# Two narrow steps in front, the top network in chunks, and another order of GpSimd's products and gathers

## The reference

```python
e = stack([tbl_f[ids[:, f]] for f in range(32)], axis=1)      # (1024, 32, 16)
x0 = xk = e
for W in (W0, W1, W2):                                        # (32, 32 or 64, 64)
    xk = relu(einsum('bmd,bhd,mhk->bkd', x0, xk, W))          # (1024, 64, 16)
    outs.append(sum(xk, axis=2))                              # (1024, 64)
h = concatenate(outs + [dense_ctx], axis=1)                   # (1024, 208)
h = maximum(h @ W_top1 + b_top1, 0)                           # 512
h = maximum(h @ W_top2 + b_top2, 0)                           # 256
y = h @ W_top3                                                # (1024, 1)
```

## Time and profile before

| | us |
|---|---|
| median of 3 runs (637.17 to 637.77) | 637.69 |
| the profiled execution | 638.89 |
| its span in the trace | 637.1 |
| DVE busy | 548.7 |
| PE busy | 563.1 |
| GpSimd busy | 488.3 |
| ACT busy | 302.5 |

### The profile page before, as it was taken

The page is one execution under the profiler, slowest core; times in us unless marked ns, Lnnn a source line. Parts: engine busy times, 40 slices in busy tenths (PEclk is TensorE's granted clock), DMA queues, the critical chain, the costliest instruction groups (busy, mean ns, idle before and its releaser), DMA issues.

```text
span 637.1 us, 7625 instructions
## 1 busy us (share of the span) xinstructions
PE 563.1 (88%) x2440; PEld 178.9 (28%) x2440; DVE 548.7 (86%) x330; ACT 302.5 (47%) x1359; POOL 488.3 (77%) x364
## 2 busy tenths in 40 slices
PE   0058998999999998999899999999999989999998
PEld 0012232332323232332223232323232322333332
DVE  0038998999999999999999999999999999897810
ACT  0023637354545646364535456464736454544352
POOL 6756898869888888979898788888897989584500
PEclk9997999999999999999999999999999999999999
DMA  3298857677876867686778768686868587871000
GB/s 105 39 391 312 307 200 284 240 298 263 306 274 227 295 217 270 244 299 214 297 274 306 268 238 315 211 298 215 307 213 319 225 302 266 307 284 49 1 1 0
DMA packets 52843, 151.01 MB, mean 237 GB/s; under 512 B 9697, under 2 KB 17377, under 8 KB 52802
## 3 DMA queue, kind: packets, MB, share of 16 engines
q1 hardware_dynamic: 44610, 148.40, 63.6%
q0 software_dynamic: 8192, 2.11, 2.5%
HBM read 147.33 MB, written 3.15 MB: 236 GB/s over the span
## 4 chain that ended last, share of the span: by engine, by line
DVE 36%; PE 24%; DMA 19%; issue 10%; POOL 8%; SPq 2%; ACT 1%; DVEq 0%; POOLq 0%
DVE prod L286 34%; PE y_ps L417 20%; DMA x0bc<-x_rows 15%; POOL emb L247 6%; DVE z L314 2%; DMA emb<-table,row_sb 2%; DMA x_rows<-emb 2%; POOL pool_prod L260 1%; SPq L214 1%; PE x_ps L477 1%; ACT relu L373 1%; PE x0g_ps L477 1%; PE x_ps L470 1%; PE x0g_ps L470 1%; PE x0g_ps L471 1%
## 5 line engine op out<-in xcount | busy, mean ns | idle before, releaser
L286 DVE TENSOR_TENSOR prod<-x0bc,x_ps 128x2048 f32<-128x2048 f32 (+1 forms) x252 | 456.0, 1878 | 8.6 <-ACT x_ps L368 8.6
L417 PE MATMUL y_ps<-prod,w_sb 128*64 128x512 f32 x1640 | 384.9, 599 | 27.8 <-DVE prod L286 27.8
L247 POOL DMA_INDIRECT emb<-table,row_sb x256 | 244.9, 957 | 65.5 <-issue 63.7
L260 POOL TENSOR_TENSOR pool_prod<-x0bc,x_sb 128x1024 f32<-128x1024 f32 x102 | 242.3, 2382 | 45.7 <-ACT x_sb L383 36.3
L417 PEld LDWEIGHTS y_ps<-prod,w_sb 128*64 128x64 f32 x1640 | 115.5, 137 | 280.1 <-issue 219.7
L373 ACT ACTIVATE relu<-y_ps 128x16 f32<-128x16 f32 x512 | 84.5, 287 | 144.3 <-PE y_ps L417 144.3
L368 ACT ACTIVATE x_ps<-y_ps 64x512 f32<-64x512 f32 x128 | 73.0, 570 | 78.5 <-PE y_ps L417 75.8
L417 PE MATMUL y_ps<-pool_prod,w_sb 128*64 128x512 f32 x408 | 105.0, 595 | 1.5 <-POOL pool_prod L260 1.3
L286 DVE TENSOR_TENSOR prod<-x0bc,x0g_ps 128x2048 f32<-128x2048 f32 x32 | 72.6, 2282 | 38.5 <-DMA x0bc<-x_rows 35.3
L373 ACT ACTIVATION_READ_ACCUMULATOR relu<-y_ps 128x1 f32 x512 | 84.7, 315 | 0.2
L383 ACT ACTIVATE x_sb<-relu 64x512 f32<-64x512 f32 x128 | 80.4, 628 | 3.4
(11 more groups left out here) (29 smaller groups left out, 49.2 us busy)
## 6 DMA issues: line engine op xcount, KB each, us to landing
x0bc<-x_rows SPq DMA_DIRECT2D x256, 512.0 KB, 6.8
x0g<-x_rows SPq DMA_DIRECT2D x16, 512.0 KB, 4.7
emb<-table,row_sb POOLq DMA_INDIRECT x256
x_rows<-emb SPq DMA_DIRECT2D x16, 128.0 KB, 2.1
w_sb<-w SPq DMA_DIRECT2D x2, 512.0 KB, 4.6
x_rows<-emb SPq DMA_DIRECT2D x16, 64.0 KB, 2.0
x0bc<-wt SPq DMA_DIRECT2D x1, 512.0 KB, 5.4
x0bc<-wt_a SPq DMA_DIRECT2D x1, 256.0 KB, 4.1
```

Of the source, the lines that this page charges most:

```text
L247: pool.indirect_dma_start(emb[:, turn, DIM * n:DIM * (n + 1)], None, table, bass.IndirectOffsetOnAxis(row_sb[:, at:at + 1], 0)).then_inc(g ...
L260: pool.tensor_tensor(pool_prod[:, n % POOL_RING, :], x0bc[:, slot(s, j), :], x[:], ALU.mult).then_inc(pool_products, 1)
L286: made = dve.tensor_tensor(prod[:, n % RING, 0:count, cols], tiles[:, :, cols], right.unsqueeze(1).to_broadcast([P, count, right.shape[1]] ...
L417: made = pe.matmul(ps[MAPS * h:MAPS * (h + 1), :], w, moving[:, HALF * h:HALF * (h + 1)], start=first, stop=final)
```

## The change

**Steps.** Seventeen steps instead of sixteen: two of 32 rows, then fifteen of 64 (`ROWS_OF`). Every tile, product and matmul of a step takes the step's width. The product's operands get a dimension for the half.

**GpSimd.** Step 0 has no GpSimd products (DVE takes all 16 tiles). Gathers of steps 0, 1 and 2 come first (8, 8, 16). Then each round runs layer 2 of step s and layer 1 of step s+1, with one gather of step s+3 behind each product, and the other gathers of s+3 at the end. PE's positions for these products change with it (`POOL_BEFORE`).

**Top network.** Five chunks: steps 0 to 4, 5 to 8, 9 to 12 (256 rows each), 13 to 15 (192) and 16 (64). Its weights and buffers have room of their own, and the weights are loaded behind step 1's tiles. A chunk's turn is the step behind its last (5, 9, 13, 16): ACT rearranges the sums; PE runs hidden layer 1 before layer 2 of that step, into the x0g banks, hidden layer 2 behind it, and the output behind the first group of the next step's layer 1 (in step 16 between the groups of layer 2); ACT issues the output's DMA. For the last chunk PE contracts the part of layers 0 and 1 first. Layer 2 of the last step is one activation and one DVE sum instead of 32 accumulating activations.

```diff
-STEPS = COLS // PAIR
+ROWS_OF = [32, 32] + [64] * 15
+STEPS = len(ROWS_OF)
-POOL_LAST = {STEPS - 2: (5, 4), STEPS - 1: (5, 4)}
-POOL_COUNT = [POOL_LAST.get(s, (3, 3)) for s in range(STEPS)]
-POOL_BEFORE = {3: [2, 3, 5], 4: [2, 3, 4, 5], 5: [2, 3, 4, 5, 5]}
-GATHERS_AFTER = {1: [1, 1, 8], 2: [1, 1, 4]}
+POOL_OF = {0: (0, 0), STEPS - 2: (5, 4), STEPS - 1: (5, 4)}
+POOL_COUNT = [POOL_OF.get(s, (3, 3)) for s in range(STEPS)]
+POOL_BEFORE = {(1, 0): [], (1, 3): [1, 3, 4], (1, 5): [1, 1, 3, 4, 5],
+               (2, 0): [], (2, 3): [2, 4, 6], (2, 4): [2, 3, 4, 5]}
+AHEAD = 3
...
+CHUNKS = [(0, 5), (5, 9), (9, 13), (13, 16), (16, 17)]
+FINAL = len(CHUNKS) - 1
+TURN = {end: c for c, (_, end) in enumerate(CHUNKS[:FINAL])}
...
@@ SP @@
                 load_x0g(s)
                 load_tiles(s)
+                if s == 1:
+                    for dst, src in ((wt1a_sb[:], wt1_a), (wt1b_sb[:], wt1_b), (wt2_sb[:], wt2), (wt3_sb[:], wt3),
+                                     (bt1_sb[:], bt1), (bt2_sb[:], bt2), (zt_b[MAPS:, :], dense_t)):
+                        sp.dma_start(dst, src).then_inc(mlp_in, 16)
...
@@ GpSimd @@
-            gather(0, 0, GATHERS)
+            gather(0, 0, GATHERS_OF[0])
             pool.wait_ge(rows_done, 2)
-            gather(1, 0, GATHERS)
+            gather(1, 0, GATHERS_OF[1])
+            gather(2, 0, GATHERS_OF[2])
             pool.wait_ge(w0_ready, 2)
             for s in range(STEPS):
-                layer(s, 1, x1_sb)
-                layer(s, 2, x2_sb)
+                done = layer(s, 2, x2_sb, s + AHEAD, 0)
+                if s < LAST:
+                    done = layer(s + 1, 1, x1_sb, s + AHEAD, done)
+                if s + AHEAD < STEPS:
+                    gather(s + AHEAD, done, GATHERS_OF[s + AHEAD])
...
@@ DVE @@
-                made = dve.tensor_tensor(prod[:, n % RING, 0:count, cols], tiles[:, :, cols],
-                                         right.unsqueeze(1).to_broadcast([P, count, right.shape[1]]), ALU.mult)
+                out, left = (t.rearrange("p t (h c) -> p t h c", h=2)[:, :, halves, :]
+                             for t in (prod[:, n % RING, 0:count, 0:width(s)], x0bc[:, at:at + count, 0:width(s)]))
+                right = x[:, halves, 0:half(s)].unsqueeze(1).to_broadcast(list(left.shape))
+                made = dve.tensor_tensor(out, left, right, ALU.mult)
...
@@ ACT @@
             for s in range(STEPS):
+                if s - 1 in TURN:
+                    hidden2(TURN[s - 1])
+                    output(TURN[s - 1])
+                if s in TURN:
+                    mlp_input(TURN[s], range(3))
                 if s < LAST:
                     place_x0g(s + 1)
                     square(s + 1)
                 finish(s, 1, x2_ps, x2_sb)
                 if s < LAST:
                     finish(s + 1, 0, x1_ps, x1_sb)
-                else:
-                    mlp(range(MLP_EARLY))
+                if s in TURN:
+                    hidden1(TURN[s])
+                if s == LAST:
+                    hidden2(TURN[s])
+                    output(TURN[s])
+                    mlp_input(FINAL, range(2))
                 finish(s, 2)
...
@@ PE @@
+            def hidden1(c):
+                n, first = CHUNK_ROWS[c], FIRST_ROW[CHUNKS[c][0]]
+                b = slice(first, first + n)
+                pe.wait_ge(zt_ready, inputs_after(c))
+                for j in range(H1_TILES):
+                    ps, out_f = x0g_ps[:, j // 2, CHUNK_B * (j % 2):][:, 0:n], slice(P * j, P * (j + 1))
+                    pe.matmul(ps, wt1a_sb[:, out_f], zt_a[:, 0:n], start=True, stop=False)
+                    made = pe.matmul(ps, wt1b_sb[:, out_f], zt_b[:, b], start=False, stop=True)
...
+            def output(c):
+                n = CHUNK_ROWS[c]
+                pe.wait_ge(mlp_act, PIECES_OF_CHUNK * c + H1_TILES + H2_TILES)
...
             for s in range(STEPS):
-                layer(s, 1, w1_sb)
+                layer(s, 1, w1_sb, {1: lambda: output(TURN[s - 1])} if s - 1 in TURN else {})
                 if s < LAST:
                     layer0(s + 1)
+                if s in TURN:
+                    pe.wait_ge(mlp_in, 16 * 7)
+                    hidden1(TURN[s])
+                if s == LAST:
+                    layer(s, 2, w2_sb, {2: lambda: hidden2(TURN[s]), 4: lambda: output(TURN[s])})
                 else:
-                    pe.wait_ge(mlp_in, 16 * 7)
-                    mlp(range(MLP_EARLY))
-                layer(s, 2, w2_sb)
-            mlp(range(MLP_EARLY, len(MLP)))
+                    layer(s, 2, w2_sb)
+                    if s in TURN:
+                        hidden2(TURN[s])
+            last_chunk()
```

More of the change, by code:

```diff
@@ L259, in layer @@
                         pool.wait_ge(pool_products_used, n - POOL_RING + 1)
[L260 to L264 removed]
+                    pool.tensor_tensor(pool_prod[:, n % POOL_RING, 0:width(s)], x0bc[:, slot(s, j), 0:width(s)],
+                                       x[:, 0:width(s)], ALU.mult).then_inc(pool_products, 1)
@@ L294, in layer0 @@
                     dve.wait_ge(bc_in[g], 32 * (s + 1))
-                    at = slot(s, group[0])
-                    product(before((s, 0)) + g, GROUP, x0bc[:, at:at + GROUP, :], x0g_ps)
+                    product(s, before((s, 0)) + g, group, x0g_ps)
             def layer(s, l, x):
@@ L301, in layer @@
                         dve.wait_ge(bc_in[g], 32 * (s + 1))
-                    n, at, count = before((s, l)) + g, slot(s, group[0]), len(group)
-                    tiles = x0bc[:, at:at + count, :]
+                    n = before((s, l)) + g
                     if g == 0:
@@ L352, in place_x0g @@
                     act.wait_ge(products, after((s - 1, 0)))
-                act.activation(x0g_ps[:].rearrange("p h c -> p (h c)"), x0g[:], ACT.Copy).then_inc(x0g_placed, 1)
+                act.activation(x0g_ps[:, :, 0:half(s)], x0g[:, 0:width(s)].rearrange("p (h c) -> p h c", h=2),
+                               ACT.Copy).then_inc(x0g_placed, 1)
             def square(s):
@@ L357, in square @@
                     act.wait_ge(squares_used, s)
-                act.activation(squares[:], x0g[:], ACT.Square).then_inc(squared, 1)
+                act.activation(squares[:, 0:width(s)], x0g[:, 0:width(s)], ACT.Square).then_inc(squared, 1)
             def finish(s, l, x=None, x_sb=None):
```

303 lines of the change are left out of this document (179 added, 124 removed).

## The result

The changed kernel takes 670.68 us, median of four runs (668.9 to 680.1), against 637.73 for the kernel before: 1.052 times as long, 95% interval 1.0475 to 1.056. The forecast was 620.2 in a range of 608 to 631. The profiled execution of the changed kernel is its slowest and a disturbed one (680.1 us, span 678.3, where the other three spans are 667.1 to 670.1), so losses read from its trace are too large by 8 to 11 us in all. Beside it I read the trace of e1 (664.75 us, span 663.0), the same program but for 60 bytes of padding.

The account below looks back on a forecast made before the run. DVE was taken as the bound, 34.35 us a step of 64 rows wherever nothing interrupts it. Span 637.1 - 7.3 - 6.7 + 15.0 - 18.5 = 619.6, plus 0.6 gives a median of 620.2 us, range 608 to 631.

Parts of the forecast that it names:

- Part 1, the front: Start of the span: narrow first steps bring layer 2 of step 2 to 97.5 us from 104.79, -7.3 us.
- ACT's spread follows: Step 0, after PE's layer 0 tiles end at 28.6: ACT spreads promptly, so DVE's layer 1 starts at 29.5.
- Part 2, the middle: Steady steps: gathering step s+3 in the round of s removes waits for rows before layer 0, -6.7 us.
- Part 3, the turns: Steps 5, 9 and 13: the top network's PE work delays DVE's layer 2 by 5.0 us each, +15.0 in all.
- Part 4, the end: Behind PE's last layer: 10.0 us remain instead of 28.5, -18.5; the 51.6 us of PE chain before it stay.
- 8 records at the 0.19 of their weight loads 1.5: End, behind the last layer of 64 rows: eight PE records priced at 0.19 us each, 1.5 us.
- 16 records 3.0: End, behind the last layer of 64 rows: sixteen further PE records, 3.0 us.
- the last sentence of that part: End: by the skill's 107 ns a load instead of 190, 24 loads are 2.0 us shorter and the end 8.0.
- B: Rival: PE absorbs the top network in its idle time, each turn costing 1.5 us or less; 609.7 us, chance 0.2.
- C: Rival: GpSimd sets the period, its wait of 1.5 us a step making 34.35 into 35.3; 631.6 us, chance 0.13.
- D: Rival: PE's clock stays slow in front, rising only behind step 0, +7 us; 627 us, chance 0.08.
- E: Rival: slower than before, the product's extra operand dimension costing DVE per instruction; 650.6 us at 100 ns, chance 0.06.

Follow-up runs that it names:

- e5: Changed kernel with GpSimd starting the 16 gathers of step 2 only when x1 of step 0 has been copied; 674.43 us.
- e11: Changed kernel with GpSimd's indirect gathers of all steps but the first replaced by plain DMAs of the same shape from rows in order; 634.21 us.
- e7: Changed kernel with the gathers of steps 5 to 16 left out, reusing rows already in the buffer; 648.99 us.
- e10: Changed kernel with GpSimd's indirect gathers of steps 5 to 16 replaced by plain DMAs of the same shape from rows in order; 650.89 us.
- e14: e11 with the seven loads of the top network's weights behind the tiles of step 3 instead of step 1; 630.70 us.
- e6: Changed kernel with the top network left out for the rows of steps 0 to 12, so without the three middle turns; 655.37 us.
- e3: Changed kernel with GpSimd's gathers placed as in the kernel before; 660.60 us, ratio 1.030 to the kernel before.
- e4: e3 with the offset column given 64 bytes a partition instead of 4; 662.22 us, ratio 1.034 to the kernel before.
- e8: Changed kernel with 16 steps of 64 rows and gathers placed as before, keeping only the chunked top network; 648.77 us, ratio 1.012 to the kernel before.
- e9: e8 with the first three chunks' hidden products cut into four pieces behind layer 0 of four steps; 633.58 us, ratio 0.988 to the kernel before.
- e12: Changed kernel with each step's 16 gathers spread over six GpSimd products as 3, 3, 2, 3, 3, 2; 747.25 us, ratio 1.166 to the kernel before.
- e13: e9 with each step's gathers spread over six GpSimd products as 3, 3, 3, 3, 2, 2; 737.65 us, ratio 1.152 to the kernel before.

## Why the prediction was wrong, point by point

**Part 1, the front: -7.3 forecast, +14.5 found.** DVE's first product was forecast at 24.0 and came at 24.73; the half-width pair at 1.13 us start to start held as well. Layer 1 was forecast at 29.5 and came at 43.91. The failed step is the sentence "ACT's spread follows": it took the 0.2 us of rows 11 and 12 for a place where GpSimd was in a row of 24 indirect gathers. e5 and e11 start layer 1 at 31.2 and 31.3 when that row is gone. The second failure is a size: I let rows be read back 3 to 4 us behind their store, as in the idle queue of rows 8, and they took 4.9 to 6.5. Of the 21.8 us between 97.5 and 119.3, what goes with the indirect DMAs is 8.4 (e11; the same front took 125 in e7 and e10, so up to 14), the weight loads are up to 4.8 (3.3 were in the forecast) and the rest, 8.6, is the narrow steps' own loads and scatter. Narrow steps gain 0.9 us over the kernel before even in e14 (103.9 for 104.8), and nothing in any version with real gathers.

**Part 2, the middle: -6.7 forecast.** What it said of the waits for rows is right: with e7, e10 and e11 there is no wait left in front of layer 0, and 34.35 us stand in row. The step that failed is that it took GpSimd's gathers as something that only occupies GpSimd. Between e11 and the changed kernel, whose only difference is the indirect instruction and its addresses, the middle differs by 36.8 us in the one trace and by 17.6 in e1's (511.0 and 493.4). In the kernel before, the runs are of 8 and 4 and behind a product of each layer; the run of eleven lies across both moments, x2 and x1, at which DVE needs PE's result with 1.3 us to spare. The new order did some harm by itself: with it x2 came up to 7.7 us late (e6 too), with the old places 0.8 at most (e3, e4). In time the old places give only 4 to 10 us back. The new order takes away the wait in front of layer 0 and puts late releases in its place, and the gain of 6.7 us is lost in the exchange.

**Part 3, the turns: 5.0 us each forecast.** Right without gathers: 39.65 - 34.35 = 5.3. Beside real gathers 6.2 to 7.7 (e3, e8) and up to 9.4 (e1), 5.1 to 5.8 each by e6's time.

**Part 4, the end: -18.5 forecast.** Right, in part by luck: 8.0 us behind PE's last layer for 10.0 forecast, and from layer 2 of the last but one step (617.14) to PE's end (670.3) 53.2 for the 51.6 that were to stay. The 2.0 are mostly the terms "8 records at the 0.19 of their weight loads 1.5" and "16 records 3.0": a load of 128 columns still takes 0.19 us, but they start 0.11 us apart, and the records took 1.1 and 2.0. (That is why the 8.0 of the last sentence of that part comes out.) The two misses nearly cancel: 61.2 us in all for 61.7.

**The sum.** Taken without indirect DMAs and with the weights later, the kernel has a span of 627.6 (e14); the forecast was 619.6, and of the 8.0 us between them 6.4 are the front. What GpSimd's indirect DMAs cost is best read from medians: e11 and the changed kernel are 36.5 us apart (634.21 and 670.68; the kernel before took 638.57 and 637.73 beside them). The traces give 29.9 between e11 and e1, namely 10.9 in front, 17.6 in the middle and 1.4 in the rest. The weights' place is worth 3.5 us in medians (e14 against e11). So of the 50.5 us between 620.2 and 670.7 the indirect DMAs are 36.5, the weights 3.5 and what e14 still lacks 10.5, most of it in front.

**The rivals.** B (PE absorbs the network) is wrong for turns of 7.7 us and nearly right for pieces of 1.7 (e9). C looked at GpSimd, the right engine, but for its products' times; e12 and e13 show that this limit is real and close, though not what happened. D did not happen: the clock granted to PE was 1.00 from 43.9 to 65.4, while DVE multiplied layers 1 and 2 of step 0, and where it was lower there (0.86 and then 0.71 in e11) DVE still did both layers without a wait inside. In the middle it doesn't go with the waits stretch by stretch (0.96 in the one above of 34.41 us, 1.00 in that of 41.87); the 0.89 is 10 us at the lower level, from 348.4 on, behind a pause of PE that began at 346.15, so a late release can bring a slower PE with it. E is refuted: eight products of layer 1 with the new operand form take 14.46 us, as in rows 3:

```profile
325.31 14.46 DVE L334 TENSOR_TENSOR prod<-x0bc,x_ps 128x1024 f32<-128x1024 f32 x8
```

The one rival for the slower side was thus a cost per instruction. None looked at what a moved run of gathers does to others, and no row of before could price it: its steady stretches have runs of eight and four and take 34.35 us all the same.

## What to carry to other kernels

A wait that takes 0.2 us in one place of a trace isn't worth 0.2 us everywhere: look at what the other engines issue at that moment, and take a second trace before a wait is priced (here one trace of the kernel before had fifteen late releases and the other none). A long run of indirect DMAs beside a hand-over without slack needs a price of its own. Work that is moved from the end into a steady loop must come in pieces smaller than the idle time that the second-busiest engine has in one round (pieces of 1.7 us into 1.5 to 2.6 left the middle 8.3 us longer, turns of 7.7 us 22.6). And a front with narrower steps shortens only what scales with bytes; the turnaround of a store that is read back, 4.9 to 6.5 us in a busy queue, comes once more for every step that is added.
